# Attention and a routed expert layer on one core: logits and ranks within the batch, buffers re-homed, loads paced, the first tile laced in

## The chip, the cores and the metric

The kernel runs on 1 core of one Trainium2 chip. The metric is the device time of one execution in microseconds, lower is better. The engines are named as the profile names them: PE (TensorE), DVE (VectorE), ACT (ScalarE), POOL (GpSimd), SP (SyncE). SP issues most DMAs.

## The reference

Input is x of 8 batches of 512 tokens, 256 wide (4096 tokens). It is normalised, goes through a causal attention of 16 heads of 16 features whose score is a second-order Taylor expansion of the exponential, and through a layer of 8 experts of which each token takes the two with the largest logits. Both are added to x. Cut:

```python
xn = layernorm(x)
# attention, per head: q, k, v of 16 columns; s = q.k / 4
A = tril(1 + s + s * s / 2)                  # as taylor_exp(q) . taylor_exp(k)
y = (A @ v) / A.sum(-1)                      # per head, heads joined
attn = y @ Wo.T
# experts
top_w, top_i = top_k(xn @ Wg, 2); top_w = softmax(top_w)
ffn = sum over the two e of top_w * (silu(xn @ W1[e]) * (xn @ W2[e])) @ W3[e]    # 256 -> 512 -> 256
out = x + attn + ffn
```

## The kernel before

It has two stages on one core, everything in float32 by splitting each operand into a high and a low part (three matmuls a product: high by high, low by high, high by low).

**Attention, 32 quarters.** Quarter n = 4b + qd is batch b, four heads. On PE it runs: scores(n, 0), the attend step of quarter n-1, slot_a, scores(n, 1), slot_b, scores(n, 2), slot_c. The scores go to PSUM banks 0 to 3; ACT squares them (squares0, squares1, squares2) into T0, T1, T2, which frees the banks for the next scores; POOL masks them on the diagonal; attend multiplies by v into bank 4; DVE copies it to yw (copy_yw). The slots hold single steps that share banks 5 to 7 in turn: x (transpose of xn), c (one of four projections to q and k), v (values and the 8 logits), C and T (column sums of v), t (yw back to tokens, then normalise by DVE into yn), y (transpose of yn, its high part yTh by ACT, low part yTl by DVE), o (output projection, added by DVE to x in xa), r (ranks of the tokens within the experts, a matmul on the mask Mb of the chosen experts), G (transpose of the lists). Every engine walks through the same slots in the same order and waits by semaphore; each engine works strictly in its program order.

**Routing.** DVE takes the two largest logits (top_two), places gives each token its slot in its expert's list, POOL writes the token's number there by an indirect DMA (place, 8 for each batch). tiles, experts and weights on DVE turn the counts into a table of tiles, cw into combine weights, which SP stores beside xn in DRAM. POOL then gathers lists, PE transposes them (G), glist and the semaphore v_gl follow.

**Expert stage, 71 tiles of 128 tokens.** POOL gathers a tile (xg), PE transposes it, up(t, 0) and up(t, 1) are two products with W1 and W2, ACT takes Silu, DVE multiplies, PE transposes, down(t) is the product with W3, DVE weighs, POOL adds to out by an indirect DMA.

**Weights.** W1 and W2 come as 16 units of 512 KB (load_w12(n), SP), are split by ACT into the high part (w12_high) and by DVE into the low part (w12_low); W3 comes as 8 units (load_w3, w3_high, w3_low). The attention's buffers lie over the places of the later units. UNITS = 9 units are loaded and split within the attention, in quarters qd 1 and 3 of batches 1 to 5, two of the others by DVE at the end, the rest within the first tiles.

**SP's order.** SP issues DMAs and waits in line. In iteration b it loads units 2b-2 and 2b-1, stores the first half of out of batch b-1 (after o(b-1, 0)), stores xn of batch b+2 (after norm_x(b+2)), stores the second half of out, waits until both halves have landed (out_sent) and loads x of batch b+3. DVE's work on batch b+2 (stats, rsqrt, norm_x) stands at the end of quarters qd 0, 1 and 2 of batch b. After iteration 7: five unit loads, cw, the W3 loads, the last two unit loads and the last out stores.

Lines: scores 872, attend 890, steps 901 to 966, squares0, squares1, squares2 at 450, 458, 463, w12_high 490, w3_high 494, copy_yw 634, places 719 to 724, norm_x 602, mask 371, SP's stores 291 and 295, its loads 298 and 301.

## Time and profile before

| | |
|---|---|
| median of 3 runs | 749.3 us (746.01 to 751.39) |
| the profiled execution | 748.22 us |
| its span on the core | 746.5 us |
| PE busy in the span | 670.4 us, 90% |
| DVE, ACT, POOL busy | 378.3, 318.9, 337.9 us |
| mean granted PE clock | 0.967 |

How to read the rows below. A row of a timeline has: start in us, us that the instructions took together, engine, line of the kernel, operation, output<-inputs, shapes, xcount; in square brackets the idle time of the engine just before and what ended it. On the SP queue the time is that of issuing, waits included. A row of the stretches by window has: from:to in us, length, busy us (xinstructions) of PE, PE's weight loads, DVE, ACT and POOL, the granted clock of PE (1.00 is 2.4 GHz), the mean busy share of the 16 DMA engines, GB/s. A DMA's time to landing is counted from its issue and is a median when there are several.

### The profile page before, as it was taken

The page shows a single profiled execution, that of the slowest core. Times are in us where ns is not written, and L with a number is a line of the kernel's source. Part 1 is how long each engine was busy: PE and PEld are TensorE (multiplying, and loading weights), DVE is VectorE, ACT ScalarE, POOL GpSimd, SP SyncE. Part 2 cuts the span into 40 slices and gives each one's busy share as a digit, 9 for nine tenths or more (in the row PEclk, how much of TensorE's full clock was granted, in tenths as well). Part 3 has the DMA queues.
Part 4 walks back from the last instruction along what each step waited for, and adds up shares of the span by engine and source line. Part 5 has one row for each costly group of instructions (what it writes and reads, how often), then busy time and mean ns, then how long its engine had stood idle before and what let it go on. Part 6 is the DMA issues. An engine that isn't in the chain of part 4 may idle for free.

```text
span 746.5 us, 15613 instructions
## 1 busy us (share of the span) xinstructions
PE 670.4 (90%) x5315; PEld 502.1 (67%) x5315; DVE 378.3 (51%) x919; ACT 318.9 (43%) x468; POOL 337.9 (45%) x356
## 2 busy tenths in 40 slices
PE   3679999999998999887569999999999999999993
PEld 2435565656565655544258888888888888888882
DVE  4645656575756654354348744444444444444441
ACT  3355756566665656364237422333322333222330
POOL 1153544545352625243305655555545555545542
PEclk9899999999999999999679999999999999999997
DMA  6106053543516050003851233333333333333331
GB/s 211 37 1 86 17 32 97 40 104 38 107 31 84 16 43 16 15 2 42 252 225 29 52 59 58 58 59 58 58 54 55 51 59 59 58 54 55 58 52 21
DMA packets 37240, 46.77 MB, mean 63 GB/s; under 512 B 9520, under 2 KB 31424, under 8 KB 37168
## 3 DMA queue, kind: packets, MB, share of 16 engines
q1 hardware_dynamic: 21024, 25.71, 17.6%
q0 software_dynamic: 15712, 19.01, 15.8%
q8 instruction: 49, 0.80, 0.5%
q10 hardware_dynamic: 432, 1.06, 0.4%
q14 instruction: 23, 0.19, 0.1%
HBM read 27.50 MB, written 18.26 MB: 61 GB/s over the span
## 4 chain that ended last, share of the span: by engine, by line
PE 74%; DVE 12%; DMA 5%; issue 3%; another core or an unknown queue 2%; ACT 1%; POOL 1%; SPq 0%; DVEq 0%; POOLq 0%; ACTq 0%
PE banks L1007 26%; PE banks L1028 13%; PE banks L872 8%; PE banks L909 6%; PE banks L890 6%; PE banks L1016 4%; PE banks L953 3%; PE banks L918 3%; PE banks L938 2%; DMA lists_scr<-ids,slots 2%; DMA out<-yo,glist 2%; PE banks L996 2%; DVE yw L634 1%; DVE st L577 1%
## 5 line engine op out<-in xcount | busy, mean ns | idle before, releaser
L371 POOL TENSOR_SCALAR_AFFINE_SELECT T<-T 128x512 f32<-128x512 f32 x128 | 79.5, 637 | 173.3 <-ACT T L458 60.6
L411 POOL DMA_INDIRECT out<-yo,glist x71 | 114.1, 1607 | 81.0 <-DMA out<-yo,glist 39.0
L540 ACT ACTIVATE sTh<-banks 128x512 fp32r<-128x512 f32 x71 | 42.5, 598 | 193.6 <-PE banks L1016 193.6
L1007 PE MATMUL banks<-w12h,xgh 128*128 x284 | 118.7, 418 | 4.5 <-DVE xgl L821 4.5
L400 POOL DMA_INDIRECT xg<-xn_scr,glist x71 | 69.7, 981 | 106.7 <-DVE yo L833 94.8
L872 PE MATMUL banks<-Qs,Ks 32*128 32x512 f32 (+3 forms) x1024 | 100.5, 475 | 16.9 <-ACT T L463 8.3
L1007 PE MATMUL banks<-w12l,xgh 128*128 x284 | 112.4, 396 | 0.0
L1007 PE MATMUL banks<-w12h,xgl 128*128 x284 | 112.3, 396 | 0.0
L826 DVE TENSOR_TENSOR sTl<-banks,sTh 128x512 fp32r<-128x512 f32 x71 | 49.0, 691 | 116.7 <-ACT sTh L540 116.7
L450 ACT ACTIVATE T<-banks 128x1024 f32<-128x1024 f32 x64 | 62.0, 1021 | 53.1 <-PE banks L872 49.0
L872 PEld LDWEIGHTS banks<-Qs,Ks 32*128 32x128 f32 x1024 | 46.0, 187 | 51.6 <-issue 21.1
L379 POOL DMA_INDIRECT lists_scr<-ids,slots x64 | 66.4, 1037 | 29.1 <-issue 14.6
L458 ACT ACTIVATE T<-banks 128x1024 f32<-128x1024 f32 x64 | 62.0, 1021 | 41.0 <-PE banks L872 28.9
L890 PE MATMUL banks<-T,vau 128*17 128x512 f32 (+3 forms) x1024 | 77.5, 443 | 0.0
L890 PEld LDWEIGHTS banks<-T,vau 128*17 128x17 f32 x1024 | 27.1, 99 | 57.9 <-issue 57.7
L1007 PEld LDWEIGHTS banks<-w12h,xgh 128*128 128x128 f32 x284 | 54.2, 191 | 12.0 <-issue 5.1
L1007 PEld LDWEIGHTS banks<-w12h,xgl 128*128 128x128 f32 x284 | 53.6, 189 | 12.1
L833 DVE TENSOR_SCALAR yo<-banks,xg 128x256 f32<-128x256 f32 x71 | 34.3, 483 | 47.9 <-PE banks L1028 41.4
L1007 PEld LDWEIGHTS banks<-w12l,xgh 128*128 128x128 f32 x284 | 54.3, 191 | 6.4
L844 DVE TENSOR_TENSOR hs<-banks,hs 128x512 f32<-128x512 f32 x71 | 49.1, 691 | 14.1 <-PE banks L1007 4.7
L1028 PE MATMUL banks<-w3h,sTh 128*128 x284 | 51.2, 302 | 0.8 <-ACT sTh L540 0.8
L1028 PE MATMUL banks<-w3h,sTl 128*128 x284 | 45.8, 283 | 0.1
(157 smaller groups left out, 1133.4 us busy)
## 6 DMA issues: line engine op xcount, KB each, us to landing
w12r<-w SPq DMA_DIRECT2D x16, 512.0 KB, 8.2
xn_scr<-xb SPq DMA_DIRECT2D x8, 512.0 KB, 9.3
out<-xa SPq DMA_DIRECT2D x16, 256.0 KB
w3r<-w SPq DMA_DIRECT2D x8, 512.0 KB, 7.0
xa<-x SPq DMA_DIRECT2D x7, 512.0 KB, 4.4
xg<-xn_scr,glist POOLq DMA_INDIRECT x71, 2.8
out<-yo,glist POOLq DMA_INDIRECT x71, 3.8
lists_scr<-ids,slots POOLq DMA_INDIRECT x64
```

What stands on the lines that cost most here:

```text
L371: e.affine_select(out=v, in_=v, pattern=[[0, 4], [1, P]], compare_op=ALU.is_ge, fill=-1.0, base=0, channel_multiplier=-1).then_inc(s["g_mk ...
L379: e.indirect_dma_start(table, bass.IndirectOffsetOnAxis(slots[:, k, blk:blk + 1].bitcast(U32), 0), ids[:, blk:blk + 1], None).then_inc(s[" ...
L400: e.indirect_dma_start(xg[:, t % GR, :], None, xn_d, bass.IndirectOffsetOnAxis(glist[:, t:t + 1].bitcast(U32), 0)).then_inc(s[f"d_g{t % GR ...
L411: e.indirect_dma_start(out, bass.IndirectOffsetOnAxis(glist[:, t:t + 1].bitcast(U32), 0), yo[:, t % 2, :], None, compute_op=ALU.add).then_ ...
L450: e.activation(T0[:, n % 2, 2 * h:2 * h + 2, :], banks[:, 2 * h:2 * h + 2, :], ACT.Square, scale=0.25, bias=1.0).then_inc(s["a_s"], 1)
L458: e.activation(T1[:, 2 * h:2 * h + 2, :], banks[:, 2 * h:2 * h + 2, :], ACT.Square, scale=0.25, bias=1.0).then_inc(s["a_s"], 1)
L826: e.tensor_tensor(sTl[:], banks[:, 5, :], sTh[:].bitcast(F32), ALU.subtract).then_inc(s["v_st"], 1)
L844: e.tensor_tensor(hs[:], banks[:, 2 * (t % 2) + 1, :], hs[:], ALU.mult).then_inc(s["v_mu"], 1)
L872: i = e.matmul(banks[:, r, c0:c0 + w], Ks[rr, g, h, jm * P:(jm + 1) * P], Qs[rr, g, q0:q0 + w], start=True, stop=True)
L890: i = e.matmul(banks[32 * r:32 * r + HA, 4, 512 - w:512], vau[:, b % 2, jm, 4 * qd + r, :], v[:, r, :], start=(jm == 0), stop=(jm == 2), s ...
L1007: i = e.matmul(banks[:, 2 * (t % 2) + m, :], a[:, k, :], w[:, bass.ds(expert[t] * 4 + (2 * k + m), 1), :], start=(k == 0 and n == 0), stop ...
L1028: i = e.matmul(banks[:, 6 + t % 2, 0:256], a[:, k * P:(k + 1) * P], w[:, bass.ds(expert[t] * 4 + k, 1), :], start=(k == 0 and n == 0), sto ...
```

## The change

- **Slots.** x(b+1) stays in qd 1; c(b+1, 0) moves from slot_b of qd 2 to slot_c of qd 1, c(b+1, 1) from qd 3 to qd 2, c(b, 3) from slot_b of qd 1 to slot_c of qd 0. All four v steps of batch b+1, with the logits, stand in slot_c of qd 2 (they were in qd 2 and 3), o(b-1, 1) and r(b+1) in slot_c of qd 3 (o was in qd 2, r in the next qd 0). G is in quarter 30 instead of 31.
- **Routing.** top_two is split: top(b+1, 0) at the end of qd 2, top(b+1, 1) in qd 3. POOL's scatters follow the ranks (places_with). tiles stands in quarter 28, experts in 29, weights in 30 (was 29), Exp in 28 (was 29).
- **Layer norm ahead.** stats(b+2) at the end of qd 1, rsqrt and norm_x(b+2) at the end of qd 3; root(b+2) in qd 2.
- **Weights.** 11 units are loaded and split within the attention, in the quarters that W12_WITH names, by ACT and DVE. Loads 11 to 13 and W3's are spread over SP's program with waits; in the first tiles ACT converts units 11 to 15.
- **SP's order.** In iteration b: loads of units 2b-2, 2b-1, first half of out, second half of out, xn of b+2, out_sent, x of b+3.
- **Buffers.** Almost all attention buffers get other addresses: each lies over a weight unit that is needed late enough (W12r and W3r are the raw places, W12h and W3h the high parts). Sizes are the same.
- **First tile.** The steps y(7, 1), o(7, 0), o(7, 1) come after transpose_g(0) and between the two halves of up(0).

The diff, cut to its core ("..." marks what is left out; the address table, which is long, is left out but for some lines):

```diff
-UNITS = 9
+UNITS = 11
 W12_BY_POOL = (12, 14)
+W12_WITH = {(1, 0): 0, (1, 2): 1, (2, 0): 2, (2, 2): 3, (3, 0): 4, (3, 2): 5, (4, 0): 6, (4, 2): 7, (6, 2): 8,
+            (7, 1): 9, (7, 2): 10}
...
@@ slot_b(n)
     elif qd == 1:
-        steps.append(("c", b, 3))
-        if b < LAST:
-            steps += [("x", b + 1, 0), ("x", b + 1, 1)]
+        steps += [("x", b + 1, 0), ("x", b + 1, 1)] if b < LAST else []
     elif qd == 2:
-        if b < LAST:
-            steps.append(("c", b + 1, 0))
+        steps += [("c", b + 1, 1)] if b < LAST else []
     else:
         steps.append(("y", b, 0))
-        if b < LAST:
-            steps.append(("c", b + 1, 1))
@@ slot_c(n)
     if qd == 0:
-        return ([("y", b - 1, 1)] if b else []) + [("r", b, 0)]
+        return ([("y", b - 1, 1)] if b else []) + [("c", b, 3)] + ([("r", 0, 0)] if b == 0 else [])
     if qd == 1:
-        return [("o", b - 1, 0)] if b else []
+        return ([("o", b - 1, 0)] if b else []) + ([("c", b + 1, 0)] if b < LAST else [])
     if qd == 2:
-        steps = [("o", b - 1, 1)] if b else []
-        return steps + ([("v", b + 1, 0)] if b < LAST else [])
-    return [("v", b + 1, i) for i in (1, 2, 3)] if b < LAST else [("G", 0, 0)]
+        return [("v", b + 1, i) for i in range(4)] if b < LAST else [("G", 0, 0)]
+    return ([("o", b - 1, 1)] if b else []) + ([("r", b + 1, 0)] if b < LAST else [])
+
+def places_with(n):
+    b, qd = divmod(n, 4)
+    if b == 0 and qd in (1, 2):
+        return ((0, 4 * qd - 4, 4 * qd),)
+    if qd == 3 and b < LAST:
+        return ((b + 1, 0, 4 if b + 1 == LAST else 3),)
+    if b == LAST:
+        return ((b, 4, 8),) if qd == 0 else ()
+    if b and qd < 2:
+        return ((b, 3 + 3 * qd, min(6 + 3 * qd, 8)),)
+    return ()
...
+        T0 = [w3_lo(2 * u, 2 * u + 2).take(f"T0{u}", 2048, F32, (4, 512)) for u in range(2)]
+        xa = [w12_lo(n).take(f"xa{i}", 1024, F32, (4, D)) for i, n in enumerate((8, 10, 13, 15))]
+        yTh = w12_hi(14).take("yTh", 1024, F32R, (2, 512))
...
@@ sync_program
             for b in range(NBATCH):
                 if b == 1:
                     e.wait_ge(s["v_wa"], 3)
-                if 1 <= b < 6:
-                    for n in (2 * b - 2, 2 * b - 1):
-                        if n < UNITS:
-                            load_w12(n)
+                if 1 <= b < 5:
+                    load_w12(2 * b - 2)
+                    load_w12(2 * b - 1)
+                if b == LAST:
+                    e.wait_ge(s["p_qk"], 4 * NBATCH)
+                    load_w12(11)
+                    load_w12(12)
                 if b:
                     store_out(b - 1, 0)
+                if b == LAST - 1:
+                    e.wait_ge(s["p_v"], 4 * NBATCH)
+                    e.wait_ge(s["d_z"], 32)
+                    e.wait_ge(s["d_tab"], 48)
+                    load_w12(9)
+                if b == LAST:
+                    e.wait_ge(s["v_cw"], 1)
+                    e.dma_start(cwo, cw[:]).then_inc(s["d_cw"], 16)
+                if b:
+                    store_out(b - 1, 1)
                 if b + 2 < NBATCH:
                     store_xn(b + 2)
                 if b:
-                    store_out(b - 1, 1)
+                    out_sent(e, b - 1)
                     if b + 3 < NBATCH:
-                        out_sent(e, b - 1)
                         e.dma_start(xa[(b + 3) % 4][:], xin[b + 3]).then_inc(s[f"d_x{(b + 3) % 4}"], 16)
-                if b == LAST:
-                    e.wait_ge(s["p_qk"], 4 * NBATCH)
-                    for n in range(UNITS, 14):
-                        load_w12(n)
-            e.wait_ge(s["v_cw"], 1)
-            e.dma_start(cwo, cw[:, 0]).then_inc(s["d_cw"], 16)
+                if b == 5:
+                    load_w12(8)
+                elif b == 6:
+                    load_w12(10)
             e.wait_ge(s["p_av"], NQ - 1)
             load_w3(0)
             load_w3(1)
+            load_w12(13)
             e.wait_ge(s["p_av"], NQ)
-            for n in range(2, 7):
-                load_w3(n)
+            load_w3(2)
+            store_out(LAST, 0)
+            store_out(LAST, 1)
+            load_w3(3)
+            e.wait_ge(s["a_th"], 2)
+            load_w3(4)
             e.wait_ge(s["p_t"], NQ)
-            load_w3(7)
+            load_w3(5)
+            e.wait_ge(s["a_th"], 3)
...
+            load_w3(6)
+            e.wait_ge(s["p_o"], 2 * NBATCH)
             load_w12(14)
+            e.wait_ge(s["a_th"], 4)
+            load_w3(7)
+            out_sent(e, LAST)
             load_w12(15)
-            store_out(LAST, 0)
-            store_out(LAST, 1)
@@ scalar_program, between squares0 and squares1
-                if 1 <= b < 6 and qd in (1, 3) and 2 * b - 2 + qd // 2 < UNITS:
-                    w12_high(2 * b - 2 + qd // 2)
-                if b < NBATCH - 2 and qd == 1:
+                if (b, qd) in W12_WITH:
+                    u = W12_WITH[b, qd]
...
+                    w12_high(u)
+                if b < NBATCH - 2 and qd == 2:
                     root(b + 2)
...
+            e.activation(warm[:, 0:1], pf[:, 0:1], ACT.Silu)
             expert_x(0)
-            e.wait_ge(s["p_o"], 2 * NBATCH)
-            e.wait_ge(s["d_o2"], 64)
-            e.wait_ge(s["a_warm"], 1)
+            w3_high(0)
+            step("y", LAST, 1)
@@ vector_program
-                if n and qd == 0:
-                    top_two(b)
...
+                elif qd == 3 and b < LAST:
+                    top(b + 1, 1)
                 for item in slot_b(n) + slot_c(n):
                     step(*item)
                 if b < NBATCH - 2:
-                    (stats, rsqrt, norm_x, lambda _: None)[qd](b + 2)
-                if 1 <= b < 6 and qd in (1, 3) and 2 * b - 2 + qd // 2 < UNITS:
-                    w12_low(2 * b - 2 + qd // 2)
+                    if qd == 1:
+                        stats(b + 2)
+                    elif qd == 3:
+                        rsqrt(b + 2)
+                        norm_x(b + 2)
+                if qd == 2 and b < LAST:
+                    top(b + 1, 0)
+                if (b, qd) in W12_WITH:
+                    w12_low(W12_WITH[b, qd])
...
@@ tensor_program, after the quarters
+            e.wait_ge(s["v_yw"], NQ)
+            transpose_g(0)
+            step("y", LAST, 1)
             e.wait_ge(s["v_te"], 1)
-            e.wait_ge(s["v_yw"], NQ)
             e.wait_ge(s["a_s"], 5 * NQ)
+            expert_of(0)
+            up(0, 0)
+            step("o", LAST, 0)
+            up(0, 1)
+            step("o", LAST, 1)
+            transpose_g(1)
             for m in range(3):
                 e.wait_ge(s[f"m{m}"], USED[m])
```

## Rows read from the trace of the kernel before

**Rows 1.** The page, part 1: busy us (share of the span) xinstructions of PE.

```profile
PE 670.4 (90%) x5315; PEld 502.1 (67%) x5315; DVE 378.3 (51%) x919; ACT 318.9 (43%) x468; POOL 337.9 (45%) x356
```

**Rows 2.** Stretches by window (columns above): changeover, expert tiles.

```profile
360.00:370.00 10.00, 6.24 (x43) 1.90 (x41) 3.75 (x6) 1.62 (x2) 3.61 (x5) 0.51 0.95 251
...
480.00:560.00 80.00, 80.00 (x493) 69.74 (x492) 35.61 (x65) 24.60 (x50) 42.94 (x35) 1.00 0.35 57
```

**Rows 3.** Timeline of PE, 347 to 390 us (columns above).

```profile
347.03 1.14 PE L872 MATMUL banks<-Qs,Ks 32*128 32x512 f32 x8
...
355.91 0.36 PE L872 MATMUL banks<-Qs,Ks 32*128 32x128 f32 x1 [4.39 <-issue]
...
364.50 0.45 PE L966 MATMUL banks<-ident,lists 128*128 128x128 f32 x1 [3.11 <-DMA lists<-lists_scr,row]
...
364.88 4.47 PE L890 MATMUL banks<-T,vau 128*17 128x512 f32 x32
...
371.99 0.63 PE L944 MATMUL banks<-ident,yn 128*128 128x128 f32 x4 [1.10 <-DVE yn L648]
...
374.23 0.55 PE L953 MATMUL banks<-Woh,yTh 128*128 128x256 f32 x1 [1.61 <-DVE yTl L692]
...
384.01 0.79 PE L1007 MATMUL banks<-w12h,xgh 128*128 x1 [2.77 <-DVE xgl L821]
...
389.78 0.49 PE L1007 MATMUL banks<-w12h,xgh 128*128 x1 [1.20 <-DVE xgl L821]
```

**Rows 4.** Timeline of PE, quarters 8 and 9.

```profile
110.46 1.14 PE L872 MATMUL banks<-Qs,Ks 32*128 32x512 f32 x8
...
111.53 2.35 PE L890 MATMUL banks<-T,vau 128*17 128x512 f32 x32
...
117.90 0.71 PE L872 MATMUL banks<-Qs,Ks 32*128 32x256 f32 x8
...
119.76 1.14 PE L872 MATMUL banks<-Qs,Ks 32*128 32x512 f32 x8 [0.45 <-ACT T L463]
...
125.02 0.63 PE L938 MATMUL banks<-ident,yw 128*128 128x128 f32 x4 [0.77 <-DVE yw L634]
```

**Rows 5.** Timeline of ACT, quarters 8 and 9.

```profile
115.47 1.94 ACT L458 ACTIVATE T<-banks 128x1024 f32<-128x1024 f32 x2 [0.81 <-PE banks L872]
...
122.76 1.06 ACT L490 ACTIVATE w12h<-w12r 128x1024 fp32r<-128x1024 f32 x1
```

**Rows 6.** Timeline of the SP queue, 62 to 116 us.

```profile
62.58 0.38 SPq L291 DMA_DIRECT2D xn_scr<-xb  x1
...
63.00 1.49 SPq L298 DMA_DIRECT2D w12r<-w  x2
...
114.28 0.37 SPq L324 DMA_DIRECT2D xa<-x  x1
...
114.69 1.53 SPq L298 DMA_DIRECT2D w12r<-w  x2
```

**Rows 7.** DMA issues of 60:68, then of 112:120: xcount, KB each, us to landing.

```profile
w12r<-w SPq DMA_DIRECT2D x2, 512.0 KB, 11.2
...
w12r<-w SPq DMA_DIRECT2D x2, 512.0 KB, 5.4
```

**Rows 8.** Stretches by window: the DMA queues at two times.

```profile
66.00:68.00 2.00, 2.00 (x16) 1.23 (x14) 1.01 (x3) 1.57 (x3) 0.78 (x2) 1.00 0.89 15
...
118.00:120.00 2.00, 1.55 (x21) 1.11 (x25) 0.00 (x0) 1.92 (x3) 0.92 (x3) 1.00 1.00 398
```

**Rows 9.** Timeline of DVE, 120 to 141 us.

```profile
120.83 0.18 DVE L719 TENSOR_TENSOR rk<-banks,taken 128x32 f32<-128x32 f32 x1
...
122.22 1.41 DVE L577 BATCH_NORM_STATS2 st<-xa 128x6 f32<-128x256 f32 x4
...
140.21 1.37 DVE L602 TENSOR_SCALAR xb<-xa,mv,sm 128x256 f32<-128x256 f32 x4
```

**Rows 10.** Timeline of the SP queue at the changeover.

```profile
348.28 7.60 SPq L298 DMA_DIRECT2D w12r<-w  x5
```

More of the change, by code:

```diff
@@ L132, in build @@
         km = keep.take("km", 2)
+        wts = keep.take("wts", 64, F32, (2, NB))
+        pidx = keep.take("pidx", 2, I32)
+        pf = keep.take("pf", 1)
+        row = keep.take("row", 1, I32)
+        warm = keep.take("warm", 1)
         A0 = room - 49152
@@ new lines, in build @@
+        ge8 = rr.take("ge8", 64, F32, (NE, NE))
+        L = rr.take("L", 32, F32, (4, NE))
+        eq = rr.take("eq", 32, F32, (4, NE))
+        rk = rr.take("rk", 32, F32, (4, NE))
+        ix = rr.take("ix", 4)
+        taken = rr.take("taken", NE)
+        i8m = rr.take("i8m", NE)
+        i4096 = rr.take("i4096", NE)
+        tl = rr.take("tl", NE)
+        end = rr.take("end", NE)
+        of = rr.take("of", 4)
+        cw = rw.take("cw", 256, F32, (NB, NE))
+        cw2 = rw.take("cw2", 256, F32, (NB, NE))
@@ L179, in build @@
+        lists = rw.take("lists", P)
+        ones = rw.take("ones", P)
+        trib = rw.take("trib", P // 2, BF16)
+        onesb = rw.take("onesb", P // 2, BF16)
+        ids = rw.take("ids", 32)
+        Mb = rw.take("Mb", 16, BF16)
+        sf = rr.take("sf", 8, F32, (2, 4))
+        rs = Region(D0, D0 + 8192)
         wqk_r = rs.take("wqk_r", 1024, F32, (2, 512))
@@ L523, in scalar_program @@
                     step(*item)
-            for item in END:
-                step(*item)
-            w3_high(0)
-            e.wait_ge(s["v_nt"], 4 * NBATCH)
-            e.activation(sm[:, 0, 0, :], sm[:, 0, 1, :], ACT.Silu).then_inc(s["a_warm"], 1)
             def expert_x(t):
@@ L987, in tensor_program @@
             attend(NQ - 1)
-            for item in END:
-                step(*item)
+            step("t", LAST, 3)
             def transpose_g(t):
```

268 lines of the change are left out of this document (123 added, 145 removed).

## The prediction, made before the change was run

> **What bounds the kernel now.** I read the page first. PE is busy for 670 of 746.5 us [rows 1], so nothing that another engine does shows unless PE waits for it. The stretches by window say where PE does wait. In the expert tiles it does not wait at all: 80.00 busy in 80.00 us (480 to 560) at the full clock, 2.4 GHz. Where the attention ends and the tiles begin it has most of its idle time: 6.24 busy of 10 us (360 to 370), granted 0.51, which is 1.2 GHz [rows 2].
>
> So there are three stretches to judge: the steady attention loop (32 quarters n = 4b + qd of nearly 10 us), the changeover, and the expert tiles. The tiles run at PE's own pace in both kernels. I therefore take the time from the second tile's first matmul (389.78 [rows 3]) to the end, 356.7 us, as unchanged, and ask only when that matmul comes.
>
> Then the quarter itself, on PE and on ACT [rows 4, 5]. Quarter 8 starts at 110.46. PE scores (1.1 us), attends quarter 7 (2.35), scores again, works through slot_b and has its third scores at 117.90, 7.4 us in. That third group needs the two activations of squares1, which start at 115.47, 5.0 us in. If ACT starts them late, the third scores, the last squares and the next quarter are all late: the scores, squares and scores of a quarter are one chain through banks 0 to 3. ACT has about 1 us to spare between squares0 and squares1, and before the change it puts the conversion of a weight unit there (122.76, 1.06 us, in quarter 9).
>
> Last the SP queue and landings [rows 6, 7]. SP issues in program order and waits in line.
>
> **The change, part by part.**
>
> *1. Weight units 0, 2, 4 and 6 are converted a quarter earlier, and loaded later.* Both halves are in the diff, but not next to each other. ACT now converts unit 2b-2 in quarter 4b (W12_WITH), between squares0 and squares1; before it was quarter 4b+1. SP still issues load_w12(2b-2) at the head of its iteration b, behind all of iteration b-1. That iteration now ends with store_out(b-2, 1), store_xn(b+1), out_sent and the next x load. Step o(b-2, 1) moved from the end of qd 2 to the end of qd 3, and norm_x(b+1) moved from qd 2 to the end of qd 3, behind places(b). So the queue reaches the unit's load only after quarter 4b has begun, while ACT wants the unit 3 us into that quarter.
>
> I work it out for b = 2 (b = 3 and 4 are alike), with S the start of quarter 4b. PE's last step before S is r(b). DVE then has the residual add until S+0.45, the rank work of 1.4 us (120.83 to 122.22 [rows 9]), four small operations of rsqrt at about 0.2 us each, as those are, and norm_x at 1.4 (140.21 [rows 9]). That is S+4.0. SP issues store_xn there, the x load 0.4 later, and the unit's load at S+4.8. The store of the 256 KB went out at S+0.5 and I take out_sent as over.
>
> When does it land? Two rows disagree. At 62.58 the xn store and two unit loads went out together and the loads landed after 11.2 us; the queue moved 15 GB/s in 66 to 68 us with its engines nearly all busy (share 0.89) [rows 6, 7, 8]. At 114.28 an x load and two unit loads with no store among them landed after 5.4, at 398 GB/s in 118 to 120 us [rows 6, 7, 8]. After the change every one of these loads goes out behind an xn store, as at 62.58, so I take the slow one. With one more transfer ahead but not the second unit, it lands some 11.6 us after the store's issue, S+15.6; for b = 1, without residual add and x load, at S+13.6. For the bound from below I take the quick rate, 1.35 us for each 512 KB: S+10.2 and S+7.7.
>
> The price of a landing at S+15.6: conversion 1.06, squares1 halves done at 17.7 and 18.7, third scores done at 19.2, then y1 and c3, the two steps of slot_c. PE had nothing from 7.4 to 17.7, and after idle stretches of this kind the clock is at 1.2 GHz (360 to 370 us [rows 2]; the attend step takes 4.47 there instead of 2.35 [rows 3, 4]). So the 1.9 us of y1 and c3 take nearly 3: the quarter ends at S+22.1. Undisturbed it would end at S+10.0 (third scores until 8.1, then 1.9). That is 12.1 us, three times, and 10.1 for b = 1: **+46.4 us**. At the quick rate, 6.5 three times and 3.5 once: +23. Nothing covers it: the work of slot_b on PE is over 7.4 us in, which is already counted.
>
> A fit of the Trainium skill (DMA: Bandwidth & Descriptors, Anatomy of one DMA — SWDGE (gpsimd) path) speaks against the slow landing: 2.0 us plus the bytes at 436 GB/s, which is an estimate of 5.6 us for the three transfers and would put the sum near the quick case. The row of 114.28 agrees with it and that of 62.58 does not.
>
> *2. The other moves in the loop.* The same matmuls run in other slots. PE waits 0.45 us at each quarter 4b+1, because slot_c of qd 0 is too short to cover the last squares, and 0.77 for yw, which stands behind the statistics on DVE [rows 4]. Both covers become better: c3 moves into slot_c, top_two and stats leave qd 0. Against that, slot_b of qd 3 loses a c step and holds 1.0 us where squares1 lasts 2; I estimate 0.6 lost. Over some seven batches **-4 us**, with 0 and -8 as ends. The POOL scatters move along with the ranks and stay three to a quarter; masks still have 4 us to spare.
>
> *3. The changeover.* Quarter 31 starts at 347.03; the second tile's up matmuls at 389.78, so 42.75 us [rows 3]. In it PE waits 4.4 us while SP pushes five unit loads (348.28 [rows 10]) and all engines stand still, 3.1 for the lists, and more for the chain yw, yn, yTh, yTl and for xgl. After the change the lists come a quarter earlier: ranks of batch 7 in quarter 27, scatters in 27 and 28, the list gather in 29, G in 30. So the last attend waits only for its own masks. It stands at the end of the quarter; with one as long as quarter 8, 9.3 us [rows 4], I put it at 9.2. From there to y1 took 7.1 with the attend at 4.47, so 5.0 at full clock: y1 at 14.2. The gathers wait for the cw store, issued when weights() ends, about 3 us into quarter 31, and are there at about 12.
>
> What is late next is a load: ACT does w3_high(0) before yTh of (7, 1), and w3 unit 0 is issued only once the store of o(6, 1) has landed. That add is done at 8.8, the store lands near 12.3, the load 4.1 later (5.4 less one transfer), conversion to 17.5, yTh and yTl 1.9 more: o(7, 0) at 19.4. The first half of up(0) is done in the gap. From the first o matmul (374.23) to the second tile (389.78) it was 15.6 us [rows 3]. Of these some 4.5 fall away, the first tile's transposes, xgh and xgl between the last o matmul and up(0) (2.77 of them idle before 384.01 [rows 3]), and half of up(0), some two fifths of the 5.8 from 384.01 to 389.78, 2.2. That leaves 8.8: second tile at 28.2. Gain 42.75 - 28.2: **-14.6 us**. If the load held nothing up and the clock stayed up, 22 and -20.7; if the out store crawls like that at 62.58, o(7, 0) is 7 later and it is -8.
>
> *4. The rest.* Warm-up of Silu, Exp a quarter earlier, buffers re-homed: no instruction more, in slots where ACT has room. The queue after the first tiles is late by design, but unit 15 and w3 rows 7 have two tiles (9.8 us) each: nothing.
>
> The sum: the profiled execution took 748.2 (span 746.5), 1.1 under the median of 749.3. 748.2 + 46.4 - 4 - 14.6 = **776 us**.
>
> **Rivals.**
>
> *A, the queue is quick behind the stores.* Same waits, but +23: 748.2 + 23 - 4 - 14.6 = 752.6. For it: the row of 114.28. Against it: the trio at 62.58 is exactly the one that returns.
>
> *B, faster.* The place is the changeover: it yields its whole 20.7 us and the loop its 8, and the four waits stay short. They decide from 5 us a quarter: with 3.5 each, as the quick case gives for b = 1, it is 748.2 + 14 - 8 - 20.7 = 733.5; with the quick case's 23 it is 742. Against it: an x load and an xn store stand ahead in three of four.
>
> *C, the queue crawls at the end too.* The out store before w3 unit 0 then meets gathers and cw: 7 us more, 783; and engines standing still as at 350 us would add up to 6: 789.
>
> **How the numbers follow.** Forecast (slow landings, 766 to 782) 0.60; A 0.15; B 0.08; C 0.17. The range leaves out B, A's lower half and the far end of C: 753 to 789. About 1% (7.5 us) is what a measurement here tells from no change: faster over 1% is B, 0.08; within 1% (742 to 757) most of A, 0.14; slower the rest, 0.78.
>
> **What would show it.** In the profile after, ACT waits for w12r at L490 in quarters 4, 8, 12 and 16 and nowhere else, each time 4 to 12 us, PE idles before its third scores there, and the clock falls. If landings after those issues are near 5 us, A is right. Without any wait for w12r in these quarters step 1 is wrong altogether. Step 3 is right if G waits for nothing, if the last attend is not behind it, and if y1's activation waits for w3r. The tiles should still be PE-bound, with 356.7 us from the second on.

## The result, and the profile after

The changed kernel takes 820.2 us (median of 4 runs, 807.5 to 831.1) against 749.7 (746.0 to 751.4). Two of the four, 825.6 and 831.1, are in a slower state that a program meets now and then, and the ratio leaves them out: 1.083 times as long, 95% interval 1.072 to 1.093. It is slower, as forecast, but by 62 us (70 between the medians) and not by 27, and outside the range of 753 to 789. The profiled execution is the quickest of the four, 807.48 us (span 805.5), so the traces explain 59.3 us, against the profiled 748.22 of before.

The page of the kernel after: PE has 24 us more busy time (lower clock, not more work) than in [rows 1], and the median unit load lands after 13.3 us, where it was 8.2.

```profile
PE 694.7 (86%) x5315; PEld 511.4 (63%) x5315; DVE 376.6 (47%) x917; ACT 319.6 (40%) x470; POOL 335.2 (42%) x357
...
w12r<-w SPq DMA_DIRECT2D x16, 512.0 KB, 13.3
```

The same three stretches in both kernels, by window: the attention up to quarter 31, the changeover up to the second tile, the tiles. Columns: length, then busy us (instructions) of PE, PEld, DVE, ACT and POOL, granted clock, DMA share, GB/s. First after:

```profile
20.90:421.22 400.32, 321.99 (x3017) 193.72 (x3017) 185.25 (x574) 188.34 (x226) 140.97 (x189) 0.92 0.27 42
421.22:448.74 27.52, 21.75 (x165) 12.76 (x165) 12.37 (x26) 10.79 (x15) 6.83 (x9) 0.88 0.39 120
448.74:805.50 356.76, 344.15 (x2114) 299.75 (x2114) 169.40 (x291) 113.75 (x221) 184.94 (x140) 0.99 0.36 64
```

then before:

```profile
20.90:347.03 326.13, 294.62 (x3028) 181.79 (x3028) 185.87 (x578) 187.83 (x224) 143.06 (x188) 0.97 0.29 45
347.03:389.78 42.75, 25.09 (x155) 15.51 (x154) 13.01 (x22) 10.67 (x14) 7.53 (x10) 0.72 0.78 220
389.78:746.50 356.72, 343.96 (x2114) 299.68 (x2114) 169.52 (x291) 113.73 (x222) 184.82 (x140) 0.99 0.33 53
```

So +74.2 us in the attention, -15.2 in the changeover, nothing in the tiles. Quarters 4, 8, 12 and 16 took 20.0, 26.8, 24.8 and 26.8 us instead of 8.9, 9.3, 9.3 and 9.3: +61.6. The other +12.6 is what remains of gains and losses in the rest.

Quarter 8 after, on PE, ACT, SP and POOL (start, us, engine, line; in brackets the idle time before and what ended it), to be laid beside [rows 4, 5]:

```profile
124.12 1.14 PE L912 MATMUL banks<-Qs,Ks 32*128 32x512 f32 x8 [1.63 <-ACT T L500]
...
145.27 2.14 PE L912 MATMUL banks<-Qs,Ks 32*128 32x256 f32 x8 [11.69 <-ACT T L495]
...
122.47 0.60 ACT L523 ACTIVATE yTh<-banks 128x512 fp32r<-128x512 f32 x1 [2.47 <-PE banks L993]
...
143.25 1.06 ACT L527 ACTIVATE w12h<-w12r 128x1024 fp32r<-128x1024 f32 x1 [12.56 <-DMA w12r<-w]
...
128.00 0.37 SPq L313 DMA_DIRECT2D xn_scr<-xb  x1
128.41 0.51 SPq L358 DMA_DIRECT2D xa<-x  x1
128.96 1.60 SPq L320 DMA_DIRECT2D w12r<-w  x2
...
125.95 0.96 POOL L420 DMA_INDIRECT lists_scr<-ids,slots  x1 [1.19 <-DVE slots L758]
127.21 0.97 POOL L420 DMA_INDIRECT lists_scr<-ids,slots  x1 [0.30 <-issue]
128.49 0.96 POOL L420 DMA_INDIRECT lists_scr<-ids,slots  x1 [0.30 <-issue]
```

The store goes out at S+3.9 and the unit's load at S+4.8, both as forecast. The unit is there only at S+19.1. ACT waits 12.56 us for it, PE 11.69 for ACT. Quarters 12 and 16 are like it (waits of 10.96 and 12.84 us). Quarter 4 (72.08 to 92.12) is not: there ACT waits only 2.82 us for its unit, because PE, ACT and DVE have stood before that for 4 to 7 us, released by nothing that the trace shows ("issue", "remote"):

```profile
83.28 1.87 PE L912 MATMUL banks<-Qs,Ks 32*128 32x384 f32 x12 [4.23 <-issue]
83.52 0.23 ACT L517 ACTIVATE Cs<-banks 128x68 f32<-128x68 f32 x1 [7.39 <-remote]
...
86.57 1.06 ACT L527 ACTIVATE w12h<-w12r 128x1024 fp32r<-128x1024 f32 x1 [2.82 <-DMA w12r<-w]
```

I call such a stretch a standstill below. The waits of the whole kernel (us in total, times, longest):

```profile
ACT w12h L527 <- DMA w12r<-w: 39.2, 4, 12.8
PE banks L912 <- ACT T L495: 35.1, 14, 12.0
...
DVE yw L668 <- remote: 27.6, 9, 5.1
...
ACT yTh L523 <- PE banks L993: 17.3, 7, 2.5
```

Three small scatters of list places (128 numbers of 4 bytes each) leave POOL within 4 us, right upon this burst. At the burst of 114.28 in [rows 6] the last one had been issued 12.8 us before (101.48).

### The profile page after: what moved, and what is told of

Same layout as the page of the kernel before. It is cut to its first block, busy times and chain, and to the rows that moved or that the text cites. A ratio compares the mean times of both kernels' runs of the same rounds, so it can differ in the third digit from the quotient of the medians.

```text
span 805.5 us, 15625 instructions
## 1 busy us (share of the span) xinstructions
PE 694.7 (86%) x5315; PEld 511.4 (63%) x5315; DVE 376.6 (47%) x917; ACT 319.6 (40%) x470; POOL 335.2 (42%) x357
## 3 DMA queue, kind: packets, MB, share of 16 engines
q1 hardware_dynamic: 21024, 25.71, 16.5%
q0 software_dynamic: 15712, 19.01, 14.6%
## 4 chain that ended last, share of the span: by engine, by line
PE 71%; DMA 12%; DVE 5%; ACT 4%; issue 4%; another core or an unknown queue 2%; POOL 1%; SPq 1%; DVEq 0%; POOLq 0%; ACTq 0%
PE banks L1046 23%; PE banks L1067 12%; PE banks L912 10%; PE banks L930 7%; DMA w12r<-w 7%; PE banks L949 5%; PE banks L1055 4%; PE banks L993 3%; PE banks L958 3%; ACT T L495 3%; DMA out<-yo,glist 2%; PE banks L1035 2%; DMA lists_scr<-ids,slots 1%; PE banks L978 1%
## 5 line engine op out<-in xcount | busy, mean ns | idle before, releaser
L912 PE MATMUL banks<-Qs,Ks 32*128 32x512 f32 (+3 forms) x1024 | 119.1, 493 | 54.4 <-ACT T L495 35.1
L912 PEld LDWEIGHTS banks<-Qs,Ks 32*128 32x128 f32 x1024 | 54.1, 192 | 98.7 <-ACT T L495 46.7
L420 POOL DMA_INDIRECT lists_scr<-ids,slots x64 | 63.0, 985 | 22.5 <-issue 14.7
L930 PEld LDWEIGHTS banks<-T,vau 128*17 128x17 f32 x1024 | 26.6, 98 | 61.6 <-issue 59.1
L1046 PEld LDWEIGHTS banks<-w12h,xgh 128*128 128x128 f32 x284 | 54.0, 190 | 10.2 <-issue 3.3
L726 DVE TENSOR_TENSOR yTl<-banks,yTh 128x512 fp32r<-128x512 f32 x16 | 11.1, 692 | 87.8 <-ACT yTh L523 87.8
## 6 DMA issues: line engine op xcount, KB each, us to landing
w12r<-w SPq DMA_DIRECT2D x16, 512.0 KB, 13.3
```

The source lines that it names most:

```text
L420: e.indirect_dma_start(table, bass.IndirectOffsetOnAxis(slots[:, k, blk:blk + 1].bitcast(U32), 0), ids[:, blk:blk + 1], None).then_inc(s[" ...
L912: i = e.matmul(banks[:, r, c0:c0 + w], Ks[rr, g, h, jm * P:(jm + 1) * P], Qs[g][rr, q0:q0 + w], start=True, stop=True)
L930: i = e.matmul(banks[32 * r:32 * r + HA, 4, 512 - w:512], vau[b % 2][:, jm, 4 * qd + r, :], v[:, r, :], start=(jm == 0), stop=(jm == 2), s ...
L1046: i = e.matmul(banks[:, 2 * (t % 2) + m, :], a[:, k, :], w[:, bass.ds(expert[t] * 4 + (2 * k + m), 1), :], start=(k == 0 and n == 0), stop ...
```

## The experiments

They came in six groups, each on a chip of its own together with the kernel before. That kernel's median went from 759 to 786 us on these chips, so only numbers of one group are compared.

### Group 1: what the four waits are worth

On this chip the kernel before took 766.9 us.

**Units loaded a batch ahead** (the conversion stays in quarter 4b; units 0 and 1 go out in batch 0):

```diff
-                if 1 <= b < 5:
-                    load_w12(2 * b - 2)
-                    load_w12(2 * b - 1)
...
                 if b:
                     store_out(b - 1, 0)
+                if 1 <= b < 4:
+                    load_w12(2 * b)
+                    load_w12(2 * b + 1)
```

> The changed kernel with one thing altered on the SP queue: in iteration b the loads of units 2b and 2b+1 (one batch ahead) stand right behind the first half of out, and those of 2b-2 and 2b-1 at the head are gone. Theory W (ACT's waits for the units cost the time): the four long quarters of 20, 27, 25 and 27 us fall to about 12 us like quarter 20, which has no unit to wait for; span 805.5 - 50 = about 755, no wait of ACT for w12r within the attention. Rival Q (the crawling queue and what it does to the engines costs the time, whoever waits): the loads crawl elsewhere, quarters 4, 8, 12, 16 stay above 17 us, span above 785.

Measured: 781.1 us, 1.020 [1.015, 1.025]. No wait for a unit is left in the attention and quarters 8, 12, 16 take 9.6 us. Quarter 4 stays at 20.6, though no unit is loaded in it and none is waited for: it is a standstill (ACT 8.1 us, PE 4.8), with an xn store and scatters in flight. And the third quarters (10, 14, 18, 22) now take 11.8, 16.3, 16.8 and 14.5: a unit issued there lands after 14.0 us, and ACT and DVE stand for 3.6 us, released by nothing that the trace shows. Quarter 30 waits 7.25 us for the lists.

**Conversion back in quarters 4b+1 and 4b+3** (W12_WITH keys (b, 0), (b, 2) to (b, 1), (b, 3)):

> The changed kernel with units 0 to 7 converted one quarter later (qd 1 and 3, as before the change); the queue as changed. Theory W: unit 2b-2 lands 19 us after quarter 4b begins, quarter 4b+1 begins at 12 and wants it 3 us in, so ACT still waits some 3 to 4 us in quarters 9, 13 and 17 and not at all in 5; quarters 4, 8, 12, 16 fall to 12; span about 770. Rival Q: above 785. If the unit lands at 15 in a queue that runs beside working engines: 757.

Measured: 797.1 us, 1.036 [1.030, 1.043]. The waits fall to 24.1 us in three, longest 11.1, and move to quarters 9, 13 and 17 (19.0, 16.9, 22.9). Quarter 4 takes 22.4 without a wait for a unit.

**y(b, 0) behind o(b-1, 1)**, in slot_c of the fourth quarter instead of slot_b:

```diff
-        steps.append(("y", b, 0))
...
-    return ([("o", b - 1, 1)] if b else []) + ([("r", b + 1, 0)] if b < LAST else [])
+    return ([("o", b - 1, 1)] if b else []) + [("y", b, 0)] + ([("r", b + 1, 0)] if b < LAST else [])
```

> The changed kernel with step y(b, 0) moved from slot_b of qd 3 to slot_c, behind o(b-1, 1). Theory Y: ACT's yTh of y(b, 0) must wait until o(b-1, 1) has read the same buffer; behind that activation in ACT's order stand the last squares of quarter 4b+3, so PE idles 1.6 us before each quarter 4b+4. Moved, that idle time goes: 7 times 1.6 = 11 us, ratio to the kernel before some 1.5% below that of the changed kernel, span about 794. Rival: PE's own work or the load waits fill the gap, span stays within 3 us of 805.

Measured: 826.6 us, 1.080 [1.075, 1.085]. The fourth quarters fall from 10.60 to 9.33 us, as expected. The time does not fall: the waits for the units are longer (54.3 us in four), and around quarter 8 the units land 16.2 us after issue instead of 14.3. How much of that is the edit and how much this chip is not shown, since the changed kernel itself did not run here.

**The first and the third together, and the norm_x store behind the C matmuls** (a wait for `p_c` ahead of store_xn):

> The changed kernel with three alterations: loads one batch ahead, y(b, 0) behind o(b-1, 1), and SP waits for the C step of batch b+1 (semaphore p_c) before it stores xn of batch b+2. Theory B: the gaps of 0.4 us between the C matmuls and DVE's late yw at the start of a batch come from the burst that SP issues just then; issued behind C, quarters 4b last 10 us rather than 12. Then 755 - 11 - 14 = about 730 of span, below the kernel before. Rival: the gaps have another cause and stay, 744; or the burst hits what follows C as hard as C, 744 too.

Measured: 766.6 us, 1.004 [1.000, 1.008]: level with the kernel before. Most of the loss is gone; what is left stands in few places, the largest in quarter 4 (20.8 us, again a standstill without a unit to wait for) and in quarter 30 (19.8):

```profile
381.37 0.45 PE L1007 MATMUL banks<-ident,lists 128*128 128x128 f32 x1 [12.18 <-DMA lists<-lists_scr,row]
```

There the list gather waits for the last scatters (16.4 us). What slowed the scatters and loads I did not know at this point.

### Group 2: the chip, and the transfers alone

**The kernel before on another chip:**

> The kernel before, unchanged, for a second trace of it on the chip of these runs: its median was 749.7 us on the first chip and 766.9 on the second. If the difference lies in crawling transfers and in the stretches where all engines stand still (near 54, 301 and 350 us), the quarters beside an xn store are longer and the plain ones equal to 0.1 us; if the chip is slower as a whole, all quarters are longer in proportion.

Measured, in a single execution: 778.7 us against 749.7 on the first chip. Of the quarters 0 to 30, 14 agree to 0.1 us. Of the 30 us between the two traces 16 sit in five quarters that stand still: 2, 6, 20, 24 and 27 take 16.0, 15.3, 14.0, 13.6 and 17.8 us. Another 8 come after quarter 31 has begun. Quarter 2 (timeline of all engines):

```profile
47.41 0.97 POOL L379 DMA_INDIRECT lists_scr<-ids,slots  x1 [0.16 <-issue]
...
48.69 0.97 POOL L379 DMA_INDIRECT lists_scr<-ids,slots  x1 [0.31 <-issue]
49.95 0.96 POOL L379 DMA_INDIRECT lists_scr<-ids,slots  x1 [0.30 <-ACT T L450]
49.97 1.15 PE L872 MATMUL banks<-Qs,Ks 32*128 32x384 f32 x16
56.31 0.69 DVE L634 TENSOR_TENSOR yw<-banks,CT 128x512 f32<-128x512 f32 x1 [8.64 <-remote]
56.44 1.94 ACT L458 ACTIVATE T<-banks 128x1024 f32<-128x1024 f32 x2 [6.72 <-remote]
57.16 1.09 PE L938 MATMUL banks<-ident,yw 128*128 128x128 f32 x4 [6.04 <-DVE yw L634]
```

Three scatters, and then PE, DVE and ACT all stand until 56.3.

**Only the transfers, on idle engines:**

> No part of the computation: only DMAs of the kernel's own shapes on idle engines, in 14 groups one after the other, each group issued at once and waited for: xn store (512 KB, rows 1056 bytes apart), the same store with rows 1024 bytes apart, the half out store, x load, unit loads, three POOL scatters. It asks what makes the queue crawl. Theory P (pitch: the rows of xn, 1056 bytes apart, are written badly and block what follows): xn store + two unit loads takes 11 us or more to land, the store at 1024 and the out store + two unit loads 5 to 6. Theory M (any store in flight with other transfers): all three take 11. Theory E (the busy engines are part of it): none crawls here, every group lands at 350 to 400 GB/s, 1.5 MB within 6 us.

Measured: no crawl. Two units behind an xn store landed after 6.2 and 6.3 us; with an x load too, 5.6; two units beside three scatters, 4.1. The scatters themselves needed 7.3 to 8.0.

### Group 3: busy engines or scatters

The kernel before took 786.0 us on this chip.

> The changed kernel itself on this chip, as the level for the next two. Theory A (the units' loads under the activations' wait set the length of quarters 4, 8, 12 and 16): those quarters take 20 to 27 us and the ratio to the kernel before is 1.07 to 1.10 on this chip too. Theory G (the C matmuls at a batch's start run with gaps because the burst of loads is issued just then): quarters 20, 24 and 28 are over 12 us and the C matmuls show gaps of 0.4 us each. Rival (the gaps belong to the chip of the first comparison): quarters 20 to 28 take about 10.3 us here, and the ratio is nearer 1.07.

Measured: 841.3 us, 1.075 [1.064, 1.085]. Quarters 4, 8, 12, 16 took 23.2, 29.0, 29.9 and 30.3; quarters 20, 24 and 28 13.7, 16.6 and 19.3, so the loss at the batch starts belongs to the kernel.

**The transfer group beside busy engines:**

> A kernel that leaves out the whole computation: twelve times the same group of transfers (norm_x store, x load, two units; in five of them three scatters of places beside it), each time beside another set of busy engines: none, TensorE alone (64 matmuls of 32 rows by 512 columns in fp32), ScalarE alone (squares out of PSUM), VectorE alone, GpSimd alone, all four. Idle engines gave 5.6 us for the second unit's landing. Theory E (an engine's work is part of the crawl): in one of the sets the units land after more than 9 us, and that set names the engine. Rival F (the crawl has to do with the long straight instruction streams of the real kernel, not with the engines' operands): all sets stay at 5 to 7 us.

Measured, the units' median landing: none busy 5.8, TensorE 6.4, ScalarE 5.7, VectorE 5.7, GpSimd 5.9, all four 6.4. With three scatters beside: none busy 14.7, TensorE 14.5, the sets with the others 10.7 to 11.3. DMA issues of the first phase, then of the one with scatters and every engine idle (xcount, KB, us to landing):

```profile
wa<-w SPq DMA_DIRECT2D x2, 512.0 KB, 5.8
xn_scr<-xb SPq DMA_DIRECT2D x1, 512.0 KB, 3.4
...
wa<-w SPq DMA_DIRECT2D x2, 512.0 KB, 14.7
xn_scr<-xb SPq DMA_DIRECT2D x1, 512.0 KB, 3.7
...
lists_scr<-ids,idx POOLq DMA_INDIRECT x3, 12.4
```

Theory E falls: engines add 0.6 us at most. In this probe the scatters make the crawl, together with a burst of 2 MB; the smaller groups of the first probe passed quickly beside them. Each set ran once.

**Scatters moved to the second and third quarter, in fours:**

```diff
-    if qd == 3 and b < LAST:
-        return ((b + 1, 0, 4 if b + 1 == LAST else 3),)
...
-    if b and qd < 2:
-        return ((b, 3 + 3 * qd, min(6 + 3 * qd, 8)),)
+    if b and qd in (1, 2):
+        return ((b, 4 * qd - 4, 4 * qd),)
```

> The changed kernel with one thing else: GpSimd's scatters of list places are issued in the second and third quarter of a batch alone, so that in batches 1 to 6 none is in flight when the burst of norm_x store, x load and two units is issued at a batch's start. Theory S (the small scatters beside the burst are what makes the queue crawl): the units land 6 to 8 us after issue instead of 13, the four waits of the activations for a unit fall from about 12 to 5 us, and the kernel is 25 us faster than the changed kernel on this chip (ratio to before about 1.04). Rival (the scatters are bystanders): waits of 11 to 13 us, time within 1% of the changed kernel.

Measured: 866.8 us. The four executions spread from 858.9 to 885.5, and the two quickest are 19 us above the changed kernel's median. Half of theory S held: in quarters 8, 12 and 16 the two units landed 5.0 to 5.3 us after issue, and the four waits fell from 49.3 to 23.9 us. The other half did not: in quarter 4 the units took 12.0 us and the xn store (75.80) 11.3, though the last scatter had gone out at 62.27; in quarter 16 the xn store took 10.3 us, its last scatter 10.5 us before it, while no engine did anything for 7 us. So the crawl and the standstill can also come when no scatter has just been issued, and quarters 4, 8, 12 and 16 still took 21.9, 19.1, 23.3 and 26.3 us. And quarters that had been plain now stood: 7, 18, 23 and 27 took 19.0, 23.7, 17.6 and 21.9 us. Quarter 18, POOL and DVE:

```profile
294.44 0.96 POOL L420 DMA_INDIRECT lists_scr<-ids,slots  x1 [0.16 <-issue]
295.71 0.97 POOL L420 DMA_INDIRECT lists_scr<-ids,slots  x1 [0.30 <-issue]
296.99 0.96 POOL L420 DMA_INDIRECT lists_scr<-ids,slots  x1 [0.30 <-issue]
298.25 0.95 POOL L420 DMA_INDIRECT lists_scr<-ids,slots  x1 [0.30 <-issue]
...
305.53 0.17 DVE L705 COPY L<-banks 128x8 f32<-128x8 f32 x1 [12.31 <-remote]
```

No large transfer was queued from 286 us on, and still everything stood, until 7 us after the fourth scatter. Loads of program code are not it either: the profile has none between 285 and 308 us.

**The level version with the same move, and units 11 and 12 behind the lists:**

> The version with units loaded a batch ahead, the second batch half of y behind o, and the norm_x store behind the C matmuls, which stood at the time of the kernel before; now also with the scatters of list places moved as in the run beside it, and with units 11 and 12 loaded only once the lists' gather has landed. Theory L (in that version the last batch lost 12 us because the gather of lists waited for scatters that stood behind three units and an out store): quarter 30 falls from 19.8 to about 9 us, and the kernel is 1 to 1.5% faster than the one before (ratio 0.985 to 0.99). Rival 1 (scatters are slow anyway): quarter 30 stays above 15 us and the ratio is 1.00. Rival 2 (units 11 and 12 are then late in the expert stage): quarter 30 is short, but a wait for w12r of over 5 us appears after the attention, ratio 1.00.

Measured: 818.9 us, 1.047 [1.039, 1.056]. Neither theory: quarter 30 took 15.1, and quarters 4, 8, 11, 16, 18, 22, 27 and 28 took 15.4 to 22.1. The scatters in fours are the common part of both losses; that they cause them is inferred here.

### Group 4: no scatters at all

The kernel before took 764.1 us here. In all three runs the 64 scatters are left out, so the lists hold spare rows and the expert stage works on those; the attention is computed in full:

```diff
-                for i in range(i0, i1):
-                    k, blk = i // 4, 4 * b + i % 4
-                    e.indirect_dma_start(table, bass.IndirectOffsetOnAxis(slots[:, k, blk:blk + 1].bitcast(U32), 0),
-                                         ids[:, blk:blk + 1], None).then_inc(s["d_sl"], 16)
```

> The kernel before, but the 64 small scatters of list places are left out (so the lists hold spare rows and the expert stage works on those; the attention is computed in full). Theory S (the standstills of 4 to 8 us follow the scatters): quarters 2, 6, 19, 20, 24 and 27 fall to the plain 8.8 to 10.4 us, and the attention stage ends at 330 to 340 us whatever the chip, 10 to 35 us earlier than with them. Rival (the standstills come from elsewhere): the same quarters stay long, the last quarter starts at 345 us or later.

> The changed kernel without the 64 scatters. Theory S: the units land 6 to 8 us after issue, quarters 8, 12 and 16 fall from 25 to 30 us to 17 to 19 us (landing 7 us after issue at 4.8 us into the quarter, plus 7.7 us of conversion and what follows it), the gaps in quarters 20 to 28 vanish, and the last quarter starts at 360 to 375 us instead of 421 to 454 us. Rival B (the burst of store, x load and two units crawls by itself): the units still land after 11 us or more, quarters 8, 12 and 16 stay above 22 us. Even under theory S the changed kernel stays slower than the kernel before without scatters by 25 to 35 us in the attention stage, since the four activations still wait.

> The version with units a batch ahead, y behind o and the norm_x store behind the C matmuls, without the 64 scatters. Theory S: no quarter above 13 us apart from the first and the fourth, last quarter starts at 345 to 350 us, and by the changeover's gain of 15 us it beats the kernel before without scatters by 0 to 1.5%. Rival: early loads still bring crawling quarters of 14 us or more in the third quarters, ratio to the kernel before without scatters above 1.01.

Measured: 720.6 us, 762.9 us and 723.9 us. The scatters cost the kernel before 43.5 us (0.944 [0.939, 0.949]). By stretch, the kernel before without scatters (columns as above):

```profile
21.30:330.20 308.90, 289.54 (x3028) 177.97 (x3028) 185.13 (x578) 187.87 (x224) 76.93 (x124) 0.98 0.14 47
330.20:361.88 31.68, 22.48 (x154) 14.65 (x154) 13.23 (x22) 10.61 (x14) 7.94 (x10) 0.78 0.89 297
```

and the changed kernel without them:

```profile
20.70:376.95 356.25, 310.30 (x3017) 188.37 (x3017) 186.14 (x575) 188.19 (x226) 78.05 (x124) 0.93 0.14 47
376.95:407.50 30.55, 24.16 (x165) 14.33 (x165) 12.23 (x25) 10.68 (x15) 7.50 (x9) 0.79 0.36 108
```

Its waits, and the landing around quarter 8:

```profile
ACT w12h L522 <- DMA w12r<-w: 26.8, 4, 7.9
```

```profile
w12r<-w SPq DMA_DIRECT2D x2, 512.0 KB, 7.0
```

The core of theory S came in: the units land 5.8 to 7.0 us after issue, in all four quarters. Its sizes did not all: the last quarter starts at 376.95 and not by 375, and the attention is 47 us longer than that of the kernel before without scatters, not 25 to 35. Quarters 4, 8, 12, 16 take 16.5, 19.7, 19.1 and 18.0; quarters 20 and 24 take 9.6. In the kernel before no quarter is left above 10.5 but 0 and 29. This trace is of an execution of 769.8 us, 7 above the run's median, and 3.5 us of that are in its tiles. The third run is about level with the first (723.9 to 720.6), not ahead. Its quarter 31 starts 9.8 us later (340.0 against 330.2), and its changeover takes 24.5 us against 31.7, so the changeover's gain shrinks from 15 us to 7 there.

### Group 5: the scatters one at a time

The kernel before took 778.1 us here. Its eight scatters of a batch go out singly, one inside the masks and one behind them in each quarter, instead of three in a row (the last batch keeps four and four):

```diff
-                    if qd < 3:
-                        place(b, 3 * qd, min(3 * qd + 3, 8))
...
+    if qd == 0:
+        return (((b - 1, 7, 8),) if b else ()), ((b, 0, 1),)
+    return ((b, 2 * qd - 1, 2 * qd),), ((b, 2 * qd, 2 * qd + 1),)
```

> The kernel before, with its scatters of list places issued one at a time: one between the second and third mask and one behind the fourth mask of each quarter, instead of three behind the fourth mask of three quarters (the last batch keeps four and four). Without them the kernel before took 720.6 us where it took 764.1 with them. Theory T (three within 4 us overfill something, single ones pass): the standstills go, and the time is 0.95 to 0.97 of the kernel before. Rival N (each scatter has its price, 0.7 us on average): same within 1%. Rival M (a scatter ahead of the third mask delays the masks, and attend waits for them): 1 to 2% slower, with a wait of PE for GpSimd in every quarter.

> The version with units a batch ahead, y behind o and the norm_x store behind the C matmuls, with the same spacing of the scatters. Without scatters it stood at 1.005 of the kernel before without scatters. Theory T: time 0.95 to 0.97 of the kernel before. Rival N: 1.00 to 1.04 of the kernel before, as its two forms with scatters on two chips; third quarters of 14 us and more stay.

Measured: 745.6 us, 0.960 [0.955, 0.966], for the kernel before with spaced scatters, and 748.6, 0.966 [0.958, 0.974], for the level version. Both beat the kernel before. Quarter 2 again, spaced:

```profile
47.79 0.96 POOL L382 DMA_INDIRECT lists_scr<-ids,slots  x1 [0.16 <-issue]
...
50.35 1.15 PE L883 MATMUL banks<-Qs,Ks 32*128 32x384 f32 x16
50.49 0.69 DVE L645 TENSOR_TENSOR yw<-banks,CT 128x512 f32<-128x512 f32 x1 [2.43 <-PE banks L901]
51.43 0.66 PE L949 MATMUL banks<-ident,yw 128*128 128x128 f32 x4
51.53 1.94 ACT L469 ACTIVATE T<-banks 128x1024 f32<-128x1024 f32 x2 [1.43 <-PE banks L883]
```

It takes 8.35 us instead of 16.0 on the chip of group 2 and 13.8 in the first comparison. Of the quarters 1 to 30 only 24 (13.6) and 29 (13.2) are above 11. Spacing does not cure the crawl: two units behind an xn store with single scatters beside them landed after 11.9 us in 56 to 72 us. Nobody waits for them there.

### Group 6: the changed kernel with single scatters

The kernel before took 759.3 us here. The edit is that of group 5, two scatters in each quarter of a batch.

> The changed kernel with its scatters of list places spaced singly, two to a quarter in all four quarters of a batch (the last batch as it was); nothing else differs. If standstills are what it lost beyond its four waits, quarters 20, 24 and 28 fall to about 10 to 11 us and the time to about 1.02 to 1.03 of the kernel before. If the crawl of the burst stays with a single scatter beside it, the four waits for units stay at 8 to 12 us each. Rival: spacing helps only a kernel that has no such waits, ratio 1.06 or more.

Measured: 790.1 us, 1.038 [1.033, 1.044]. Quarters 20, 24 and 28 take 10.5, 10.1 and 10.2, quarters 8, 12, 16 21.0, 19.5 and 20.8, and the four waits stay (35.7 us in all). Quarter 4 (28.5, with a standstill of ACT of 7.6 us ahead of a wait of 9.9 for the unit) and quarter 30 (19.1, the lists again) are what keeps it from 1.02. The ratio compares with the kernel before as it was, and that one gains 4.0% by the same spacing. With both spaced the change costs 44.5 us (790.1 against 745.6, on two chips). So spacing helps both kernels, and most of the loss stays.

## Why the prediction was half right

**Right: where.** ACT waits for w12r in quarters 4, 8, 12 and 16 and nowhere else, PE idles before its third scores, the clock falls (0.76 over quarter 8). The issue times S+4.0 and S+4.8 hold. The tiles take 356.8 us where 356.7 was assumed. The early loads, which take these four waits away and move the loads off the batch's start, brought it to 1.020 of the kernel before, where the changed kernel stands at 1.075 to 1.083 on other chips.

**Right by luck: quarter 4.** It came out at 20.0 us where 20.1 was forecast. But only 2.82 us of it are a wait for the unit, and it took 20.6, 20.8 and 22.4 us in three runs that wait for no unit there. A standstill fills it, which the forecast did not have.

**Mis-sized: the landing, "S+15.6".** It was S+19.1 in quarter 8, 14.3 us after issue. The four quarters cost +61.6 us, not +46.4. They are 12.0 us longer than forecast (98.4 against 86.4); the other 3.2 are the sum's own slip, as it counted from an undisturbed quarter of 10.0 where the kernel before had 36.8 in all four. The two rows that disagreed, 11.2 and 5.4 us [rows 7], I told apart by the xn store. That was the wrong mark: store, x load and two units take 5.7 to 6.4 us beside any busy engine or none, and 14.7 with three scatters beside. Around 62.58 two scatters went out (61.49 and 62.76), before 114.28 the last at 101.48. A fit of the Trainium skill (DMA: Bandwidth & Descriptors, Anatomy of one DMA — SWDGE (gpsimd) path), stated there for a DMA issued from GpSimd, gives an estimate of 5.6 us for three transfers and 6.8 for four. The four transfers from SP took 5.8 us in the probe and 7.0 in the kernel without scatters, near that estimate, and 14.7 with scatters in the probe, far from it. So the change would have met the quick queue, had there been no scatters: 7.0 us from issue to landing without them, and +36.6 us for the four quarters (73.3 against 36.8). Even that is more than rival A's +23. But scatters in flight are not the whole mark: in the run with the scatters moved, a store crawled 13.5 us after the last one, longer than the 12.8 us before the quick burst of 114.28. What decides there is open.

**The step that failed: "The POOL scatters move along with the ranks and stay three to a quarter".** It was counted as free. Moving the ranks to the end of a batch put the scatters at 125.95 to 129.45, onto the burst at 128.00 to 130.56, once a batch. The whole attention shows it: +74.2 us with scatters, +47.3 without (356.25 against 308.90). So of the loss in the attention 27 us is what the scatters cost beyond their cost before, nearly all of it (25.0) in the four quarters. This subtracts runs on different chips; quarters without a standstill agree between chips, standstills do not, so 27 is good for the size only. Pairs on one chip point the same way: the change costs 42.3 us without scatters (762.9 against 720.6) and 55.4 as it is (62 in the first comparison). They differ by less than 27, because the changeover gains more with scatters than without. With single scatters in both kernels the cost is 44.5 us, on two chips. So about two thirds of the loss stay without the scatters: the late loads and the steps that now wait.

**Wrong sign: "The other moves in the loop", -4 us.** Without scatters, what is left outside the four quarters is 47.3 - 36.6 = +10.8. The third quarters grow by 0.77 each (10.27 against 9.50; they now hold all four v steps), the fourth by 0.62. The idle 0.45 before quarter 4b+1 went; but 1.63 came before quarter 4b, as the rows at 122.47 and 124.12 show: o(b-1, 1), moved behind the squares, still reads the buffer that y(b, 0) of the same quarter overwrites, so yTh waits for o and the last squares stand behind yTh on ACT. The run with y behind o took 1.27 us off each of these quarters. I had looked at which work covers a wait, and not at who reads the buffer.

**Right in size, in part by luck: the changeover, -14.6.** It is -15.2, and the second tile comes 27.5 us after quarter 31, forecast 28.2. Two misses cancel in it: the first matmul of o(7, 0) comes at 21.4 instead of 19.4, and from there to the second tile it is 6.1 us instead of 8.8. The order of steps is as told: the load of w3 holds up ACT, then yTh, then o:

```profile
438.84 0.79 PE L1046 MATMUL banks<-w12h,xgh 128*128 x1 [0.70 <-DVE xgl L857]
...
442.60 0.36 PE L993 MATMUL banks<-Woh,yTh 128*128 128x256 f32 x1 [0.84 <-DVE yTl L726]
...
440.09 1.06 ACT L531 ACTIVATE w3h<-w3r 128x1024 fp32r<-128x1024 f32 x1 [1.96 <-DMA w3r<-w]
```

But without scatters the gain is smaller: 1.1 us in one trace (31.68 against 30.55), 7.2 in the other (against 24.5). The kernel before is 11.1 us shorter there without its scatters, of which the last went out at 342.55, 5.7 us ahead of the five unit loads. So a good part of the change's gain may be that it parts the two; that is inferred. The standstill "while SP pushes five unit loads" was read as the loads' doing, and the same reading cost the forecast its size in the loop. The changeover alone, without the loop's moves, was not tried.

In all: +61.6, +12.6 and -15.2 are 59.0 of the 59.3 us between the profiled executions.

## What to carry to other kernels

When two rows of the same transfer disagree, list everything that was in flight at each, small transfers first, before choosing a cause: here 4-byte scatters of 512 bytes in all decided between 5.8 and 14.7 us for 2 MB. Space small scatters out singly (4.0% for the kernel before) and keep them off the bursts, and price a moved scatter by what it will then stand beside. When a step moves past another, look for the buffer that the one reads and the other writes, and not only for the work that covers it.

## What the runs showed of the hardware that I had not expected

- After three or four scatters of 128 numbers each within 4 to 5 us, PE, ACT and DVE can each stand for 6 to 12 us with nothing large on the queues (all at once 4.7 us in quarter 2 of group 2 and 6.3 in quarter 18 of group 3). Without scatters no such stretch is left in the kernel before; with single ones, 2.5 us or more apart, few are. How a scatter stops engines that have nothing to do with it stays open: the trace names no releaser ("remote", "issue"), and in the probe TensorE beside three scatters was not held up (16.5 us for its 64 matmuls, 16.9 without them).
- The chips differ by this to a good part. The kernel before took 750 us in the first comparison and 759, 764, 767, 778, 779 and 786 us in the six groups; between its two traces on different chips 14 of 31 quarters agree to 0.1 us.
- VectorE's fourteen additions over 128x1024 took 8.5 us alone, 13.9 beside the other three engines, and 19.1 when scatters were added.
